# Scans over four head columns at once, with loads, key products and sums in pairs, in a Macaron block with gated linear attention

## The reference, cut to what matters

```python
x = x + 0.5 * ffn(layernorm(x))          # int8 weight and activations, 256 x 256, bias
x = x + attn(layernorm(x))               # below
x = x + 0.5 * ffn(layernorm(x))          # the same quantized layer again

def attn(x):                             # 16 heads, kd = 8 keys, hd = 16 values a head
    xn = rmsnorm(x, ln1_w)
    q, k, v = xn @ Wq, xn @ Wk * hd**-0.5, xn @ Wv
    gk = log_sigmoid(xn @ Wkg1 @ Wkg2 + bkg2) / 16
    g = xn @ Wg + bg
    for t in range(512):                 # per batch and head; S is kd x hd
        S = S * exp(gk[t])[:, None] + k[t][:, None] * v[t][None, :]
        o[t] = q[t] @ S
    o = silu(g) * layernorm_per_head(o)
    x = x + o @ Wo
    xn2 = rmsnorm(x, ln2_w)
    return x + (silu(xn2 @ W1) * (xn2 @ W3)) @ W2      # hidden 704
```

## Time and profile before

| what | value |
|---|---|
| median of 3 runs | 162.41 us (161.65 to 162.49) |
| span of the profiled execution | 159.7 us |
| TensorE matmul / weight load busy | 138.1 us (86%) / 108.0 us (68%) |
| VectorE busy | 124.6 us (78%) |
| ScalarE busy | 101.4 us (63%) |
| GpSimd busy | 93.1 us (58%) |
| scans (L1109), 96 of them | 47.5 us |
| key products (L555), 96 of them | 50.1 us |
| `qs` (L1122), 24 of them | 19.9 us |
| DMA, SyncE's queue | 13.73 MB, 42.8% of 16 engines |
| TensorE's granted clock in 40 slices of 4.0 us (9: 90% or more) | 9999999999759999999999999999999999999985 |

### The profile page before, as it was taken

One profiled execution on the slowest core, in us unless ns is written; L12 is line 12 of the kernel. 1 busy time (PEld: TensorE's weight loads), 2 busy tenths in 40 slices (PEclk: granted clock), 3 DMA queues, 4 the chain that ended last, 5 costly groups with the idle time before them and its releaser, 6 DMA issues.

```text
span 159.7 us, 3270 instructions
## 1 busy us (share of the span) xinstructions
PE 138.1 (86%) x907; PEld 108.0 (68%) x908; DVE 124.6 (78%) x312; ACT 101.4 (63%) x234; POOL 93.1 (58%) x212
## 2 busy tenths in 40 slices
PE   0189997993199899989999999999999999999951
PEld 0145886771186788875876778777687889897620
DVE  2888898699395999999999999998786363155674
ACT  3598799990483686957767423856691864297660
POOL 2679527467977888499987923296862010041570
PEclk9999999999759999999999999999999999999985
DMA  4689036656678988887665266300010002000003
GB/s 138 153 270 334 17 57 106 138 83 102 102 98 149 251 170 130 139 119 147 129 104 81 33 102 101 58 2 0 0 37 0 0 30 71 4 2 0 0 0 133
DMA packets 20946, 14.33 MB, mean 90 GB/s; under 512 B 3696, under 2 KB 20416, under 8 KB 20928
## 3 DMA queue, kind: packets, MB, share of 16 engines
q1 hardware_dynamic: 20512, 13.73, 42.8%
q10 hardware_dynamic: 416, 0.39, 0.7%
HBM read 4.68 MB, written 1.05 MB: 36 GB/s over the span
## 4 chain that ended last, share of the span: by engine, by line
PE 54%; DVE 10%; issue 9%; POOL 6%; ACT 6%; SPq 6%; DMA 6%; POOLq 0%; DVEq 0%; ACTq 0%
PE bank L778 25%; PE bank L942 11%; SPq L467 6%; PE bank L824 4%; POOL kv L555 4%; DVE kv L1109 3%; DMA kv<-v_sb 3%; PE bank L905 3%; PE bank L884 3%; DVE qs L1122 2%; PE bank L834 2%; DMA w_in<-L_ffn_weight 2%; PE bank L894 2%; ACT cen L642 2%; PE bank L787 1%
## 5 line engine op out<-in xcount | busy, mean ns | idle before, releaser
L555 POOL TENSOR_TENSOR kv<-kv,k_sb 128x128 f32<-128x128 f32 (+1 forms) x96 | 50.1, 546 | 16.0 <-DMA kv<-v_sb 10.6
L1109 DVE TENSOR_TENSOR_SCAN kv<-bank,kv 128x128 f32<-128x128 f32 (+1 forms) x96 | 47.5, 536 | 4.3 <-POOL kv L555 4.2
L778 PE MATMUL bank<-xT,w 128*128 128x128 f32 (+1 forms) x240 | 37.9, 311 | 0.7 <-DVE hid L1154 0.6
L778 PEld LDWEIGHTS bank<-xT,w 128*128 128x128 f32 x240 | 33.7, 191 | 3.6 <-issue 1.6
L942 PE MATMUL bank<-w,hid 128*128 128x256 f32 (+1 forms) x96 | 24.4, 393 | 0.0
L600 ACT ACT_TABLE_LOAD x17 | 21.8, 1283 | 0.3
L1122 DVE TENSOR_TENSOR qs<-kv,bank 128x512 f32<-128x512 f32 (+1 forms) x24 | 19.9, 849 | 1.4 <-PE bank L884 1.4
L942 PEld LDWEIGHTS bank<-w,hid 128*128 128x128 f32 (+1 forms) x96 | 16.9, 189 | 5.4 <-issue 3.8
L824 PE MATMUL bank<-ident,cen 128*128 128x128 f32 x64 | 13.0, 320 | 7.4 <-ACT cen L661 5.8
L824 PEld LDWEIGHTS bank<-ident,cen 128*128 128x128 f32 x64 | 8.2, 159 | 12.4 <-ACT cen L661 6.1
L581 POOL TENSOR_TENSOR xin<-x,half_bias 128x256 f32<-128x256 f32 (+1 forms) x6 | 5.4, 906 | 15.8 <-DVE x L1165 15.8
(11 more groups left out here) (111 smaller groups left out, 246.3 us busy)
## 6 DMA issues: line engine op xcount, KB each, us to landing
kv<-v_sb SPq DMA_DIRECT2D x64, 64.0 KB, 2.4
kv<-v_sb SPq DMA_DIRECT2D x32, 128.0 KB, 3.9
w<-L_attn_W SPq DMA_DIRECT2D x3, 640.0 KB, 6.8
x_in<-L_attn_x SPq DMA_DIRECT2D x4, 128.0 KB, 3.3
...
```

Source lines behind the costliest of these rows:

```text
L555: pool.tensor_tensor(slot, slot, k_sb[:, tokens(u)], ALU.mult).then_inc(kv_ready, 1)
L778: mm = pe.matmul(dst, weights[k], xT[:, k, tokens(u)], start=(k == 0), stop=(k == KC - 1))
L1109: dve.tensor_tensor_scan(slot, bank[u % 2][:, 0:T], slot, first, ALU.mult, ALU.add).then_inc(scanned, 1)
```

## The change

The unit of work along the columns grows. Loads, key products and sums take two columns at a time, `t = 0` and `t = 1` of the same c, and scans take four.

- A column's row in `kv` and `v_sb` gets one more element in front, T + 1 in all. It holds zero from the load on, and for units that continue a sequence the last state of the unit before: the new stage `carry u` (VectorE) copies those 16 elements from unit u to unit u + 1, for u = 0, 1, 3, 4. The decay at that element is zero, so one scan over four rows of T + 1 elements starts each row afresh from its own first element.
- The decay goes to SBUF, four copies of it (`decays`, written by `a`), where it was in PSUM.
- A unit has 8 loads (132 KB for 128 tokens, 263 KB for 256) where it had 16, 8 key products, 4 scans, 4 `qs` as before, and 2 `sum` of twice the columns.
- `carry u` waits for all scans of unit u and for all 8 loads of unit u + 1. Scans of a continued unit wait for `carry`.
- From unit 2 on, a load waits for the products of the unit two before (`v_sb` has room for every unit now). Units 4 and 5 take the places of units 1 and 0 in `kv`.
- Weights are arranged on the host, so that each comes in one or two DMAs: `kg`, `wv`, `wkq`, `wgo`, `w13`, `w2`, and the small vectors in one on ScalarE's queue. `w13` and `w2` (1.44 and 0.72 MB) now stand between the loads of units 0 and 1 in SyncE's list. `perm`, `gate1T` and `kg1T` are gone.
- The last hidden block has 128 rows, 64 of them zeros (`hid_last`); the matmul that clears the bank of `down` stays for the 256-token units alone.
- 14 matmuls of zeros (`warm0`) stand at the head of TensorE's list.
- The order of stages around this is the old one with the columns taken together: on GpSimd `nm 2`, `nrs 3`, `kv 1 7`, `nm 3` now follow 7 and 8 of 8 products.

```diff
     "sync": stages(
+        "x 0, x 1, wload kg, wload wv, wload wkq, x 2, x 3, x 4, x 5, wload wgo, load 0 0, load 0 2, load 0 4, "
+        "load 0 6, load 0 1, load 0 3, load 0 5, load 0 7, wload w13, wload w2, load 1 0, load 1 2, load 1 4, "
...
     "gpsimd": stages(
+        "0 6, kv 0 1, kv 0 3, kv 0 5, kv 0 7, nm 1, kv 1 0, kv 1 2, kv 1 4, kv 1 6, kv 1 1, kv 1 3, kv 1 5, nm 2, "
+        "nrs 3, kv 1 7, nm 3, xb 4, kv 2 0, xs 1 4, kv 2 2, xs 1 5, mrs 0, kv 2 4, kv 2 6, kv 2 1, kv 2 3, kv 2 "
...
     "vector": stages(
+        "decay 0, amax 1 4, norm1 2, scan 0 0, qs 0 0, ffn 1 3, moments 3, scan 0 1, qs 0 1, scan 0 2, qs 0 2, "
+        "amax 1 5, decay 1, scan 0 3, qs 0 3, carry 0, scan 1 0, qs 1 0, scan 1 1, qs 1 1, og 0, scan 1 2, qs 1 "
+        "2, on 0, decay 2, scan 1 3, qs 1 3, carry 1, res 0, ffn 1 4, og 1, on 1, scan 2 0, qs 2 0, moments 4, "
...
     "tensor": stages(
+        "warm0 14, wquant, xqT 1 0, xqT 1 1, ffn 1 0, ffn 1 1, gatew, xqT 1 2, warm 5, xnT 1 0, ffn 1 2, xnT 1 1, "
...
                 elif s[0] == "load":
+                    _, u, c = s
                     sync.wait_ge(v_ready, u + 1)
+                    if u in SHARED and c == ORDER[0]:
+                        former = SHARED[u]
+                        sync.wait_ge(qs_ready, NG * (former + 1))
+                        sync.wait_ge(carried, former + 1)
+                    if u >= 2:
+                        sync.wait_ge(kv_ready, nth_pair(u - 2, c))
+                    n = 2 * (width(u) + 1)
+                    src = values(u)[c * H:c * H + H, :, :].rearrange("p t n -> p (t n)")
+                    dst = segments(u)[:, pair(c), :].rearrange("p t n -> p (t n)")
+                    sync.dma_start(dst, src.unsqueeze(1).broadcast_to([H, KD, n])).then_inc(v_spread[u % 2][c], 16)
...
                 elif s[0] == "kv":
+                    both = segments(u)[:, pair(c), 1:T + 1]
+                    pool.tensor_tensor(both, both, k_sb[:, tokens(u)].unsqueeze(1).broadcast_to([P, 2, T]), ALU.mult
                                        ).then_inc(kv_ready, 1)
...
                 elif s[0] == "a":
-                    act.activation(a, a, ACT.Exp, scale=-1.0 / NORMALIZER).then_inc(a_ready, 1)
+                    act.activation(decay_of(u)[:, :, 1:T + 1], a.unsqueeze(1).broadcast_to([P, GROUP, T]), ACT.Exp,
+                                   scale=-1.0 / NORMALIZER).then_inc(a_ready, 1)
...
                 elif s[0] == "scan":
+                    _, u, g = s
                     if own(u).start:
-                        dve.wait_ge(scanned, nth_scan(u - 1, d))
-                        first = kv[:, batch(u), d, own(u).start - 1:own(u).start]
+                        dve.wait_ge(carried, sum(batch(v) == batch(v + 1) for v in range(u)))
                     dve.wait_ge(a_ready, u + 1)
-                    dve.wait_ge(kv_ready, nth_scan(u, d))
-                    dve.tensor_tensor_scan(slot, bank[u % 2][:, 0:T], slot, first, ALU.mult, ALU.add
+                    dve.wait_ge(kv_ready, OCT * u + 2 * (g + 1))
+                    slot = segments(u)[:, GROUP * g:GROUP * g + GROUP, :].rearrange("p s n -> p (s n)")
+                    dve.tensor_tensor_scan(slot, decay_of(u).rearrange("p s n -> p (s n)"), slot, 0.0, ALU.mult, ALU.add
                                            ).then_inc(scanned, 1)
+                elif s[0] == "carry":
+                    u = s[1]
+                    dve.wait_ge(scanned, NG * (u + 1))
+                    for c in range(OCT):
+                        dve.wait_ge(v_spread[(u + 1) % 2][c], 16 * ((u + 1) // 2 + 1))
+                    dve.tensor_copy(segments(u + 1)[:, :, 0], segments(u)[:, :, width(u)]).then_inc(carried, 1)
...
                 elif s[0] == "sum":
+                    pe.wait_ge(qs_ready, NG * u + 2 * (par + 1))
                     for i in range(GROUP):
+                        mm = pe.matmul(bank[O_BANK][32 * i:32 * i + 32, 0:2 * T], pick[:, par, :],
+                                       products(u, par)[:, 2 * i:2 * i + 2, :].rearrange("p t n -> p (t n)"),
+                                       start=(par == 0), stop=(par == 1), tile_position=(0, 32 * i))
...
                 elif s[0] == "down":
-                        pe.matmul(pb[:, :], zeros[:, :], wqT[0:1, :, :].rearrange("p k n -> p (k n)"),
-                                  start=True, stop=False)
+                        if count(u) > 1:
+                            pe.matmul(pb[:, :], zeros[:, 0:P], zeros[:, :], start=True, stop=False)
+                            h = hid[:, u % 2, rows] if c < FULL else hid_last[:, u % 2, i * P:i * P + P]
```

More of the change, by code:

```diff
@@ L182, in bank_plan @@
             idle.append(("warm", at))
-        if s[0] in ("sum", "q", "down", "warm"):
+        if s[0] in ("sum", "q", "down", "warm", "warm0"):
             continue
@@ L779, in project @@
                 return mm
[L781 removed]
             for at, s in enumerate(STAGES["tensor"]):
[L783 removed]
+                if s[0] == "warm0":
+                    pe.wait_ge(zeros_ready, 1)
+                    for _ in range(s[1]):
+                        pe.matmul(bank[ROTATING[-1]][:, :], zeros[:, 0:P], zeros[:, :], start=True, stop=True)
+                elif s[0] == "warm":
                     pe.wait_ge(wqT_ready, 1)
```

332 lines of the change are left out of this document (147 added, 185 removed), and 106 rows, old and new, of the table STAGES.

## The result

The changed kernel takes 190.49 us, the median of four runs (189.92 to 192.15), against 162.45 us for the kernel before on the same chip: 1.178 times as long, with a 95% interval of 1.170 to 1.186. The forecast was 174 us in a range of 163 to 184. So the direction was right, and the loss is 28 us where 11.6 were forecast.

A forecast was written before the change was run, and what follows sets the result against it. From 43.4 us on TensorE's summed work was taken to bound the kernel, early delays passing through. Span 159.7 + 13.1 (`carry` wait) + 2.6 (half clock) - 4 (TensorE) = 171.4, plus 2.7 to the median: 174 us, range 163 to 184.

The forecast's parts named there:

- the wait: VectorE's `carry 1` waits for all of unit 2's loads, holding `res 0` to 64.6 us: +13.1 us at `xnT 2 0`.
- the hint it rested on: Line L1087, which reads and writes SBUF, took up to 607 ns against a median of 414.
- what follows `xnT 2 0` is the sum of TensorE's work: TensorE from 43.4 us on: time is the sum of its work; early delays reach the end one for one.
- The 1.4 us for the warm-up: TensorE's start: warm-up matmuls and removed `gate1T` shorten the half-clock stretch, `v 0` at 18.9 us; bounds 0 and 4.8.
- Weights and loads of units 0 and 1: SyncE's list: unit 0's loads 7.8 us to 28.0, weights 6.4 to 34.4, unit 1's loads 7.8 to 42.2.
- From there to `nm 3`: GpSimd after `carry 0`: `kv 1 5` 0.7 us, then 2.65 plus 0.27 through `nm 3`; `norm1 3` at 45.3.
- Unit 2's loads: From `v 2` done at 46.9: 1.3 ahead, 15.6 of data at 135 GB/s, 0.6 behind; landed at 64.4 us.
- `res 0` to `xnT 2 0`: Through `sq`, `mrs` and `norm2`: 2.8 us as before, so `xnT 2 0` at 67.4 against 54.30.
- -4 of TensorE: TensorE's work: `down` clearing matmuls 1.3, 128-row blocks 1.7, about 1 us of small waits closed.
- +2.6 of clock: TensorE behind the gap of some 9 us before `xnT 2 0`: half clock again, 2.6 us; otherwise 0.
- the first rival: Loads: longer rows stream faster, from about 225 GB/s, and the carries never bind: 157 us, faster; chance 0.14.
- the second rival: VectorE's scans and GpSimd's products contend in SBUF: 2 us ahead of `nm 3`, 4 later, 180 us; chance 0.14.

The follow-up runs named there:

- The kernel with the wait alone: Changed kernel with single-column scans, decay in PSUM, no `carry` copies; VectorE still waits for all 8 loads where each `carry` stood: 182.13 us.
- the one with the last two moves: Changed kernel with single-column scans, early weights and early `nm 3`, plus `xb 5` behind `xb 4` and `v 2` ahead of `g 1`: 164.39 us, ratio 1.022.
- single scans: Changed kernel with one-column scans, decay left in PSUM and no `carry`; loads, products and sums stay in pairs: 173.8 us.
- a kernel where TensorE sets the end: Kernel before with `nm 2`, `nrs 3`, `nm 3` early on GpSimd, plus the change's `down`: 157.5 us, ratio 0.974.

## Why the prediction was wrong

The changes taken back one by one give the loss in parts. Each row is worth the difference to the row above it, once as the difference of two medians, once as that of two ratios to the kernel before on the same chip, times 161.4 us:

| taken back | time | ratio | worth by time | worth by ratio |
|---|---|---|---|---|
| the changed kernel | 190.5 | 1.178 | | |
| chained scans with the decay in SBUF | 182.1 | 1.140 | 8.4 | 6.1 |
| the wait for all loads of a unit | 173.8 | 1.079 | 8.3 | 9.9 |
| the places of the weights and of `nm 3` | 166.1 | 1.030 | 7.7 | 8.0 |
| `xb 5` behind the products, the late `v 2` | 164.4 | 1.022 | 1.7 | 1.4 |
| the rest: pairs and their order (leaves the kernel before) | 160.8 | 1.000 | 3.6 | 3.5 |

So a part is known to about 2 us, the fourth is not clear of noise, and another order of taking back could share the time out differently.

**Two causes were weighed as either-or, and both came.** The forecast summed the wait and gave the contention a place among the rivals, with 0.14 and 180 us. That is the step that failed. Nothing in the argument made them exclude each other: the wait sits ahead of `res 0`, the contention in every stretch where scans and products run together. The kernel with the wait alone ran 182.1 us, and the changed kernel 8.4 above it. The price was off as well: the rival took 2 us ahead of `nm 3` and 4 behind, on the ground that TensorE's lead and VectorE's slack would take the rest; the decay in SBUF alone cost the kernel before 10.5. And the hint it rested on, one line with 607 ns instead of 414, was a fair one: it was to weigh more.

**A second step failed with it: that what follows `xnT 2 0` is the sum of TensorE's work.** It held for the kernel before, and the forecast carried it over to the changed one, with slack on the other engines and nothing for TensorE's waits. Behind `xnT 2 0` TensorE stood 15.7 us where it had stood 6.2, and it worked 14.1 us at 1.2 GHz where it had been 1.7. Of the kernels without contention, the one with the wait stood 13.6 us there and the one with the last two moves, which has no such wait, 14.9, so most of the standing comes from neither of the two causes.

**Where the steps ran off.** The forecast's own chain to `xnT 2 0`, and what the trace has:

- `v 0`: forecast 18.9 us. The first load was issued at 20.56 (SyncE's queue):

```profile
20.56 7.95 SPq L452 DMA_DIRECT2D kv<-v_sb  x8
```

The 1.4 us for the warm-up were wrong. Its 14 matmuls ran, and the first steps behind them were quicker, four transposes in 0.63 us where the same took 1.08. But TensorE then stood for 0.19, 1.33 and 0.58 us, four transposes at 13.69 took 1.11 us, and five matmuls of 512 columns took 2.34, as long as before:

```profile
1.18 4.80 PE L752 MATMUL bank<-zeros 128*128 128x512 bf16 x14 [1.18 <-DVE zeros L929]
7.28 0.63 PE L766 MATMUL bank<-ident,w_in 128*128 128x128 f32 x4 [1.30 <-ACT w_in L587]
...
13.69 1.11 PE L789 MATMUL bank<-ident,cen 128*128 128x128 f32 x4
14.60 2.34 PE L757 MATMUL bank<-wqT 128*128 128x512 bf16 x5
```

The stretch around them lists clock 0.50 here, with the same durations as in the kernel before, where the profile listed full clock; so the prediction read those steps rightly as steps at 1.2 GHz:

```profile
14.00:17.00 3.00, 2.94 (x9) 1.14 (x7) 2.79 (x14) 1.90 (x7) 2.67 (x6) 0.50 0.00 0
```

- Weights and loads of units 0 and 1: forecast landed at 42.2, `carry 0` done at 42.9. The copy started at 42.61 and was done at 43.24. Right, though by luck, since two errors cancel in it: the start was 1.7 us late, and from there to the end of the copy it took 22.7 us where 24.0 were forecast.
- From there to `nm 3`: forecast 45.3 for `norm1 3`; it came at 47.96. 1.4 of the 2.7 us were there at the end of `kv 1 5` (43.80 where 42.4 was forecast). The other 1.2 are contention, on the path: from `nm 2` to `nm 3` it took 4.1 us (43.80 to 47.93) where 2.9 were forecast, and 2.8 with single scans.
- Unit 2's loads: forecast 17.5 us from `v 2` to the last landing; `v_sb` was done at 49.54 and the copy started at 69.59, 20.0 later. The rate of 127 GB/s against 135 accounts for 1.0 of the 2.5; the rest was not looked into.
- `res 0` to `xnT 2 0`: forecast 2.8, measured 2.5. Together +17.9 us where +13.1 was forecast.
- Behind `xnT 2 0` the forecast had -1.4 (-4 of TensorE, +2.6 of clock), and it was +11.5: 116.9 us to the end against 105.4. By TensorE's time these are +9.5 of standing, +6.2 of clock (14.1 us at 1.2 GHz against 1.7, half of the difference), and -4.2 of work. With the wait kept and the scans single it is 109.5 us, so 7.4 of the 11.5 go with the scans' form: `nm 4`, `mrs 2` and the products of unit 3 late, the hole of 3.75 us ahead of `xnT 2 2`, and the stretches of lower clock at 86.4 and 113.7 us, which that kernel doesn't have (its clock is 1.00 from 73 to 174 us).

**What was right.** The mechanism of `carry` and its place, with `res 0` the one that pays; the idle times (4.42 and 12.14 us, forecast "the second for some 10 us"); TensorE's hole of 11.78 us and the lower clock right behind it (forecast some 9 us and 2.6 lost; 5.2 us at 1.2 GHz are 2.6). The loads' rate, 127 to 132 GB/s at rows of twice the length, inside the 115 to 160 named, and with that the first rival was out. TensorE's term of -4 us as work (-4.2 behind `xnT 2 0`), though its longer standing outweighed it here; the larger part, `down` with 3, gave 2.8 to 3.5 us in a kernel where TensorE sets the end. What the prediction named as a sign of the second rival, scans over 1.4 us in units of 128, was met by the longest there, at 1.89 us, and by the products that had a scan beside them, 1.31 us on average.

**The range** reached to 184 because each cause was let happen by itself; the forecast's 174 and the rival's 6 us together give 180. The 16.4 us between forecast and result are 4.8 ahead of `xnT 2 0` (1.2 contention, 2.5 the longer run of unit 2's loads), 12.9 behind it, and -1.3 since the median lies only 1.4 us over the profiled span. Of the 12.9 us 7.4 go with the scans' form. The other 5.5 are there in the kernel with the wait alone too, where TensorE's standing grew by 7.4 us, and they were not parted further. One such wait is for `xb 5` (1.53 us on VectorE at 80.06 us in the changed kernel), which no step of the prediction had followed behind `mrs 0`.
